# Middle stage of a two-layer attention and expert kernel: shared roots, normalising split over two engines, first rows added by tile

## What is computed

```python
x = x + L0_xattn(layernorm(x), ctx)      # 16 heads of 8, gathered keys
x = x + L0_ffn(layernorm(x))             # one of 16 experts a token, capacity 256
x = x + L1_xattn(layernorm(x), ctx, ctx) # one head, causal, keys = values = ctx
x = x + L1_ffn(layernorm(x))             # dense SiLU layer + product-key experts

def layernorm(x):
    m = mean(x, -1); v = var(x, -1)
    return (x - m) / sqrt(v + 1e-5)
...
scores = einsum('bqd,bkd->bqk', query, key) * 128 ** -0.5
scores = where(tril, scores, -inf)
out = einsum('bqk,bkd->bqd', softmax(scores), value)
```

## Time and profile before

| | us |
|---|---|
| median of 3 runs | 533.6 (532.41 to 536.13) |
| the profiled execution | 534.3 |
| its span in the trace | 532.6 |
| busy TensorE, VectorE | 415.9 (78%), 376.3 (71%) |
| busy ScalarE, GpSimd | 348.5 (65%), 344.5 (65%) |
| mean granted TensorE clock | 0.885 of full speed |

### The profile page before, as it was taken

The page is one execution under the profiler, slowest core; times in us unless marked ns, Lnnn a source line. Parts: engine busy times, 40 slices in busy tenths (PEclk is TensorE's granted clock), DMA queues, the critical chain, the costliest instruction groups (busy, mean ns, idle before and its releaser), DMA issues.

```text
span 532.6 us, 9386 instructions
## 1 busy us (share of the span) xinstructions
PE 415.9 (78%) x2528; PEld 344.0 (65%) x2528; DVE 376.3 (71%) x1628; ACT 348.5 (65%) x652; POOL 344.5 (65%) x251
## 2 busy tenths in 40 slices
PE   4968897819999639788667878889778787888956
PEld 3757786509999528676456657767566665776746
DVE  4457777402232147985989999999999999999970
ACT  2362654412222226986888889988898888998884
POOL 5226777740000175630789888898888988889882
PEclk9796889769999955865989998898999999889897
DMA  7981010023777111100000000000000000000000
GB/s 208 335 219 55 21 35 21 31 74 85 217 195 214 39 55 37 54 26 1 11 10 21 10 20 10 20 20 10 20 10 20 20 10 20 10 20 20 10 11 11
DMA packets 42418, 29.71 MB, mean 56 GB/s; under 512 B 4155, under 2 KB 38555, under 8 KB 42395
## 3 DMA queue, kind: packets, MB, share of 16 engines
q1 hardware_dynamic: 38539, 22.85, 14.9%
q0 software_dynamic: 2624, 6.30, 3.5%
q10 hardware_dynamic: 1232, 0.31, 0.3%
HBM read 18.95 MB, written 8.39 MB: 51 GB/s over the span
## 4 chain that ended last, share of the span: by engine, by line
DVE 22%; POOL 15%; ACT 12%; issue 5%; PE 4%; DVEq 1%; ACTq 0%; POOLq 0%
POOL arena_sb L484 15%; DVE picked_sb L1408 10%; ACT arena_sb L720 7%; ACT L720 4%; DVE bank L1370 2%; DVE first_sb L1367 2%; PE bank L1052 1%; DVE best_sb L1396 1%; DVE first_sb L1372 1%; DVE near_sb L1375 1%; DVE arena_sb L1421 1%; ACT xh_sb L510 1%; DVE pair_sb L1391 1%; ACT sc_sb L646 1%; PE bank L981 1%
## 5 line engine op out<-in xcount | busy, mean ns | idle before, releaser
L484 POOL TENSOR_TENSOR arena_sb<-arena_sb,picked_sb 128x2192 f32<-128x2192 f32 x32 | 154.4, 4846 | 25.6 <-DVE picked_sb L1408 25.6
L1408 DVE SCALAR_TENSOR_TENSOR picked_sb<-arena_sb,best_sb,bank 128x36 f32<-128x36 f32 (+1 forms) x256 | 107.7, 493 | 1.2
L1052 PE MATMUL bank<-ident_sb,arena_sb 128*128 128x128 f32 (+1 forms) x512 | 73.2, 305 | 34.6 <-DVE arena_sb L1421 30.9
L1052 PEld LDWEIGHTS bank<-ident_sb,arena_sb 128*128 128x128 f32 (+1 forms) x512 | 66.6, 169 | 39.8 <-issue 28.2
L476 POOL TENSOR_TENSOR arena_sb<-near_sb,sim_y_sb 128x1536 f32<-128x1536 f32 x32 | 87.7, 2759 | 1.3 <-DVE near_sb L1375 1.3
L720 ACT ACTIVATE arena_sb<-arena_sb,bsum_sb 128x548 f32<-128x548 f32 x128 | 85.6, 740 | 1.0 <-POOL arena_sb L484 0.8
L449 POOL DMA_INDIRECT picked_sb<-made,made_row_sb x32 | 30.7, 961 | 78.9 <-DMA made<-arena_sb 70.0
L714 ACT ACTIVATE arena_sb<-arena_sb 128x2192 f32<-128x2192 f32 x32 | 65.3, 2042 | 0.2
L1043 PE MATMUL bank<-w_down_t_sb,h_sb 128*128 128x128 f32 x256 | 34.8, 280 | 16.0 <-DVE x_all_sb L1427 15.3
L1043 PEld LDWEIGHTS bank<-w_down_t_sb,h_sb 128*128 128x128 f32 x256 | 31.1, 192 | 18.9 <-issue 18.9
L1031 PEld LDWEIGHTS bank<-xt_sb,w_up_t_sb 128*128 128x128 f32 x256 | 33.5, 192 | 14.8 <-issue 14.8
(11 more groups left out here) (176 smaller groups left out, 866.0 us busy)
## 6 DMA issues: line engine op xcount, KB each, us to landing
w_sb<-w SPq DMA_DIRECT2D x32, 256.0 KB, 3.4
...
```

The costliest lines, as they stand in the source:

```text
L484: pool.tensor_tensor(pp[p][:, :, :], pp[p][:, :, :], picked[p][:, :, :], ALU.mult).then_inc(weighed, 1)
L1052: ins = pe.matmul(bank[4 * p][0:n, c * P:(c + 1) * P], pp[p][:, h, c * P:c * P + n], ident[:, :], is_transpose=True, start=h == 0, stop=h ...
L1408: ins = dve.scalar_tensor_tensor(out=picked[p][:, h, lo:hi], in0=vv[p][:, h, lo:hi], scalar=best[p][:, h, TOP - 1:TOP], in1=scores, op0=AL ...
```

## The change

- `combine(0)` waits tile by tile, on a semaphore for each of the first four gathers (`first_gathered`).
- Means, variances and roots of statistics 2 (block g) and statistics 3 (block g-2) lie side by side in `cmv` and `croot`, eight columns. `roots(g)` makes both with one logarithm and one exponential over 128x8 and signals `croot_ready`. It waits for `cstat2_ready` of g and `cstat3_ready` of g-2. The factor 128^-0.5 of `cscale` has gone into `centre_s`, a scaled copy of `centre` which the contexts are multiplied with.
- `last_tokens(g)` on ScalarE normalises tiles 0 and 1; a new `last_tokens(g)` on GpSimd makes the bias and then tiles 2 and 3 (`cxh_pool`). It stands where `biases3(g)` stood. PE's `last_tokens_t(g)` waits for both.

```diff
-        cbias, cscale, cve2, cve3, crstd, cnb = ([sb(f"{n}{p}", [P, BT]) for p in two] for n in "cbias cscale cve2 cve3 crstd cnb".split())
+        cmv = [sb(f"cmv{p}", [P, TT, 2]) for p in two]
+        croot = [sb(f"croot{p}", [P, TT]) for p in two]
+        cmv2, cmv3 = ([t[:, lo:lo + BT] for t in cmv] for lo in (0, BT))
+        cscale, crstd = ([t[:, lo:lo + BT] for t in croot] for lo in (0, BT))
...
-            step(pool.memset(eps_d[:, :], EPS * D))
             step(pool.tensor_scalar(centre[:, :], ident[:, :], -1.0 / D, None, ALU.add))
+            step(pool.tensor_scalar(centre_s[:, :], centre[:, :], float(D) ** -0.5, None, ALU.mult))
...
-            def biases3(g):
+                                            ).then_inc(first_gathered[n] if g == 0 else gathered[g], 16)
+
+            def last_tokens(g):
+
                 p = g % 2
-                pool.wait_ge(croot3_ready, g + 1)
+                pool.wait_ge(croot_ready, g + 3)
                 if g >= 2:
                     pool.wait_ge(cxh_ready, g - 1)
                 step(pool.tensor_tensor(cnb[p][:, :], cmv3[p][:, :, 0], crstd[p][:, :], ALU.mult))
                 pool.tensor_scalar(cnb[p][:, :], cnb[p][:, :], -1.0, None, ALU.mult).then_inc(crstd3_ready, 1)
+                hold(pool, crstd3_ready, g + 1)
+                if g >= 2:
+                    pool.wait_ge(xt3_mm, g - 1)
+                for t in range(BT // 2, BT):
+                    ins = pool.tensor_scalar(xh[p][:, t, :], x_all[:, g * BT + t, :], crstd[p][:, t:t + 1], cnb[p][:, t:t + 1],
+                                             ALU.mult, ALU.add)
+                ins.then_inc(cxh_pool, 1)
...
-                biases3(g)
+                last_tokens(g)
                 if g + 4 < NB:
                     gathers(g + 4)
...
-            def normalise(first, dst, scale, bias, done):
-                for t in range(BT):
+            def normalise(first, dst, scale, bias, done, tiles=BT):
+                for t in range(tiles):
                     ins = act.activation(dst[:, t, :], x_all[:, first + t, :], ACT.Identity,
...
-            def roots2(g):
+            def roots(g):
 
                 p = g % 2
-                act.wait_ge(cstat2_ready, g + 1)
-                step(act.activation(cve2[p][:, :], cmv2[p][:, :, 1], ACT.Ln, bias=eps_d[:, 0:1], scale=float(D)))
+                lo, hi = 0 if g < NB else BT, TT if g >= 2 else BT
+                if g < NB:
+                    act.wait_ge(cstat2_ready, g + 1)
                 if g >= 2:
+                    act.wait_ge(cstat3_ready, g - 1)
                     act.wait_ge(cbias_ready, g - 1)
-                act.activation(cscale[p][:, :], cve2[p][:, :], ACT.Exp, scale=-0.5).then_inc(crstd2_ready, 1)
-
-            def roots3(g):
-                p = g % 2
-                act.wait_ge(cstat3_ready, g + 1)
-                step(act.activation(cve3[p][:, :], cmv3[p][:, :, 1], ACT.Ln, bias=eps1[:, 0:1]))
-                if g >= 2:
-                    act.wait_ge(crstd3_ready, g - 1)
-                act.activation(crstd[p][:, :], cve3[p][:, :], ACT.Exp, scale=-0.5).then_inc(croot3_ready, 1)
+                if g >= 4:
+                    act.wait_ge(crstd3_ready, g - 3)
+                    act.wait_ge(cxh_pool, g - 3)
+                step(act.activation(croot[p][:, lo:hi], cmv[p][:, lo:hi, 1], ACT.Ln, bias=eps1[:, 0:1]))
+                act.activation(croot[p][:, lo:hi], croot[p][:, lo:hi], ACT.Exp, scale=-0.5).then_inc(croot_ready, 1)
 
             def exps(g):
                 p = g % 2
-                act.wait_ge(crstd2_ready, g + 1)
+                hold(act, croot_ready, g + 1)
...
-                normalise(g * BT, xh[g % 2], crstd[g % 2], cnb[g % 2], cxh_ready)
+                normalise(g * BT, xh[g % 2], crstd[g % 2], cnb[g % 2], cxh_ready, BT // 2)
...
             for g in range(NB - 2):
-                roots3(g)
-                roots2(g + 2)
+                roots(g + 2)
                 last_tokens(g)
...
                 probabilities_out(g + 2)
-            roots3(NB - 2)
+            roots(NB)
...
-            roots3(NB - 1)
+            roots(NB + 1)
...
-                pe.matmul(bank[(0, 2, 3, 4, 6)[n]][:, 0:hi - lo], centre[:, :], ctx_row[:, lo:hi],
+                pe.matmul(bank[(0, 2, 3, 4, 6)[n]][:, 0:hi - lo], centre_s[:, :], ctx_row[:, lo:hi],
...
+                pe.wait_ge(cxh_pool, g + 1)
...
-                dve.wait_ge(gathered[g], 16 * BT)
+                if g:
+                    dve.wait_ge(gathered[g], 16 * BT)
                 for n in range(g * BT, g * BT + BT):
+                    if g == 0:
+                        dve.wait_ge(first_gathered[n], 16)
                     ins = dve.scalar_tensor_tensor(out=tile(n), in0=made_x[:, n, :], scalar=gate[:, n:n + 1],
...
-                    dve.wait_ge(crstd2_ready, g - 1)
+                    dve.wait_ge(croot_ready, g - 1)
...
-                dve.wait_ge(crstd2_ready, g + 1)
+                dve.wait_ge(croot_ready, g + 1)
```

More of the change, by code:

```diff
@@ L102, in program @@
         eps1 = sb("eps1", [P, 1])
-        eps_d = sb("eps_d", [P, 1])
+        centre_s = sb("centre_s", [P, P])
         arena = sb("arena", [P, 4, HP * WIDE])
@@ L214, in program @@
         cc_mm, cc_ready = sem("cc_mm"), sem("cc_ready")
-        (x2_ready, cstat2_ready, crstd2_ready, cstat3_ready, crstd3_ready, cxnt_mm, cxnt_ready, csc_mm, cmax_ready, cbias_ready, cexp_ready, cpt_mm,
-         cpt_ready, co_mm, x3_ready, croot3_ready) = map(sem, (
-            "x2_ready cstat2_ready crstd2_ready cstat3_ready crstd3_ready cxnt_mm cxnt_ready csc_mm cmax_ready cbias_ready cexp_ready cpt_mm "
-            "cpt_ready co_mm x3_ready croot3_ready").split())
+        (x2_ready, cstat2_ready, cstat3_ready, crstd3_ready, cxnt_mm, cxnt_ready, csc_mm, cmax_ready, cbias_ready, cexp_ready, cpt_mm,
+         cpt_ready, co_mm, x3_ready, croot_ready, cxh_pool) = map(sem, (
+            "x2_ready cstat2_ready cstat3_ready crstd3_ready cxnt_mm cxnt_ready csc_mm cmax_ready cbias_ready cexp_ready cpt_mm "
+            "cpt_ready co_mm x3_ready croot_ready cxh_pool").split())
+        first_gathered = [sem(f"first_gathered{t}") for t in range(BT)]
         (down_mm, xt3_mm, xt3_ready, cxh_ready, sim_mm, sim_ready, score_mm, up_mm, h1_ready, near_ready, vv_ready,
@@ L668, in _ @@
             tokens_out(0)
-            roots2(0)
+            roots(0)
             exps(0)
@@ L672, in _ @@
             probabilities_out(0)
-            roots2(1)
+            roots(1)
             exps(1)
```

3 lines of the change are left out of this document (1 added, 2 removed).

## The result

| | before | after |
|---|---|---|
| median of 12 runs each | 534.06 us (531.37 to 536.13) | 536.56 us (534.02 to 538.90) |
| ratio | 1 | 1.0047, 95% interval 1.0028 to 1.0067 |
| profiled execution, its span | 534.3, 532.6 | 534.24, 532.5 |
| first gather to the last stage's first VectorE instruction | 67.06 | 68.02 |
| from there to the end | 280.83 | 279.71 |

The changed kernel is 2.5 us slower: inside 1%, where 535.5 us was forecast, and with an interval that excludes 1. The two profiled executions do not show it in their spans. The one of after is 2.3 us quicker than its own median, so it is the stage that has to be read, not the span.

The account below looks back on a forecast made before the run. No engine was taken as full; gathers arrive nearly just in time, so GpSimd's added work shows. Late gathers +2.9 less the tail's 0.9 make +2.0 us on the 533.6 median: 535.6, rounded to 535.5, range 532.3 to 539.2.

Parts of the forecast that it names:

- First rows: Start of the middle stage: block 0 taken tile by tile, so combines 1 to 3 come 0.78 us earlier.
- The constant: One added GpSimd product of 0.55 us ahead of the first barrier, 0.5 us of it hidden.
- The tile: GpSimd's two normalising products a turn, ahead of the gathers: 0.55 us each, plus 0.1 wait on its own bias.
- The landing: From a group's last gather issue to its block's combine: between 2.46 and 3.38 us, taken as 3.0.
- GpSimd's issues: Gather issues behind root, bias and tiles: GpSimd's own turn 6.77 us against 6.31, two-turn loop through the root 14.15.
- Sum at the gathers: Combines in the middle stage come late: block 4 by 1.2 us, block 6 by 2.4, block 7 by 2.9.
- The tail: After the last gather: 0.45 us back at block 7's maximum, 0.48 at block 6's last tokens, together 0.9.
- The last stage: Its first VectorE instruction comes near 253.8 us; the rest of the span, 280.8 us, stays unchanged.
- The shared root: ScalarE saves 0.43 us a turn and waits 0.62 for the bias; with 0.77 of tiles off, 0.58 freer.
- A: Rival: gathers are not late, with tiles of 0.35 us and landings of 2.5; -0.5 us, 533.1; chance 0.20.
- B: Rival: VectorE's sequence alone bounds the middle stage's turn, 6.0 us instead of 6.31; -2.9 us, 530.7; chance 0.07.
- C: Rival: GpSimd's tiles cost 1.0 us each, by contention with VectorE, its turn 7.67; +5.9 us, 539.5; chance 0.11.

Follow-up runs that it names:

- e9: The changed kernel unaltered, measured again as a reference: 536.13 us, ratio 1.0036.
- e1: The kernel before with only the first rows waited for tile by tile: 534.18 us, ratio 0.9995.
- e3: The kernel before with only half of the last normalising moved to GpSimd, two roots kept: 533.96 us, ratio 1.0001.
- e12: The changed kernel with GpSimd's half from block 4 on only, last tokens behind the exponentials, similarities first at the seam: 536.41 us, ratio 1.0034.
- e2: The kernel before with only the shared root and scaled constant, all four tiles on ScalarE: 536.89 us, ratio 1.0062.
- e5: The changed kernel with all four tiles normalised on ScalarE, none on GpSimd: 545.75 us, ratio 1.0025 within its set.
- e4: The changed kernel with gathers issued two tiles further ahead: 535.20 us, ratio 1.0035.

## Why the prediction was right, and where not

The time came out in the range, 1.1 us above the forecast. The likeliest case was the one that happened: late gathers, in every one of blocks 4 to 7. That the number came so near is luck in part. The sum put +2.0 us into the middle stage; in the profile this stage grew by 1.02, while the medians moved by 2.5. And one of its signs of being wrong, that the second start moves and the end does not, holds in the profiled execution (252.79 against 251.77, span 532.5 against 532.6); the medians and e9 say that the end does move. By its steps:

- *First rows.* Block 1 was said at 196.5 and was added at 196.54; 0.78 us, as e1 shows alone.
- *The constant.* 0.55 said, 0.549 measured. GpSimd's constants ended at 6.27 us and PE started at 6.57, still held by a load. Hidden.
- *The tile.* 0.55 taken, 0.477 in the mean of 16. The wait on its own bias was 0.21, not 0.1. So wait and pair, said at 1.20, took 1.10 (0.21 and 0.89) to 1.24 (0.21 and 1.03). In the first turn the gather behind took 1.13 instead of 1.02.
- *The landing.* 3.0 taken, 2.45 to 2.48 measured: the term most mis-sized, 0.5 us too high at each block.'s 3.38 was a real landing, but the rarer one: of the 20 additions of blocks 4 to 7 in all profiles that waited for a gather, 17 came 2.45 to 2.60 us after its issue and three later, at 3.38 (before), 3.27 (e3) and 3.18 (e12).
- *GpSimd's issues.* The last ones of groups 4 to 7 were said, by the sum, at 214.0, 220.8, 228.15 and 234.9, and came at 214.13, 220.73, 227.88 and 234.48. So the chain through root, bias, tiles and issues was right to 0.4 us. Two of its terms were somewhat high: GpSimd's own turn took 6.60 us, not 6.77, and the loop of two turns through the root 13.75, not 14.15.
- *Sum at the gathers.* Block 4 said at 217.0, came at 216.60; block 6 231.15 and 230.36; block 7 237.9 and 236.93. +2.9 said, +1.92 measured, and the landing explains half of the difference. Waits of 0.5 to 1.2 us were said and 0.23 to 0.74 came.
- *The tail.* 0.9 back, and 1.92 - 1.02 = 0.90 came. The maximum of block 7 waits 0.18 instead of 0.63, the 0.45 of the step.
- *The last stage.* Said near 253.8, came at 252.79. The rest was said unchanged at 280.8 and took 279.7; in e1 to e12 it lies between 279.6 and 280.8 us, so 1 us of a single profiled span is scatter. The stage's +1.0 and e9's +1.6 us are less than the medians' +2.5 (and +2.2 in e9); 0.7 to 1.5 us is not located.
- *The shared root.* The sum had its way through GpSimd to the gathers, which is the one that acts in the changed kernel. Its way through ScalarE and PE was missing. The prediction counted 0.43 off ScalarE, 0.62 of waiting on, and let both act only on GpSimd's chain and on ScalarE's sum ("so 0.58 us freer"). It did not follow the exponentials, PE's order and the scores behind the last tokens. Alone the root costs 0.62% (e2). In the changed kernel the half takes 0.77 us of tiles off ScalarE: the exponentials start at 209.59, 0.50 behind the addition, as in the kernel before. e5, without the half, has e2's waits back. e4, without the late gathers, still has waits of up to 1.59 at the maxima. The sum came near for this reason too, not only for those it gave: the half happened to pay what the sum had left out.

Of the rivals, A (gathers in time) had the landing right and GpSimd's turn wrong: its tile of 0.35 was too cheap. B fell with the turn. GpSimd's 6.78 was said as 6.77, but that is chance: it is the mean of two turns of 6.60 and one of 7.15 in which the root was waited for. C's price was not reached: no pair of tiles took over 1.33 us. Its mechanism, contention, is there: the pair took 0.88 or 0.89 us away from VectorE's addition of rows, beside it 1.01 to 1.03, and that addition 1.25 to 1.31 instead of 1.13. Beside VectorE's addition of the attention, which reads one of its inputs from PSUM (`bank`), neither grew:

```profile
243.20 0.89 POOL L469 TENSOR_SCALAR xh_sb<-x_all_sb,croot_sb,cnb_sb 128x128 f32<-128x128 f32 x2 [0.21 <-POOL cnb_sb L464]
...
243.24 1.12 DVE L1348 SCALAR_TENSOR_TENSOR x_all_sb<-bank,csum_sb,x_all_sb 128x128 f32<-128x128 f32 x4
```

That is in accord with the Trainium skill's GPSIMD Engine Reference (8. Key points), which names a VectorE instruction with two SBUF inputs as one case of contention. The Trainium skill's GPSIMD Engine Reference (3.1 Elementwise) gives about 0.35 us for a tile, an estimate from its cycles an element; the measured 0.44 to 0.48 decides.

The range's upper end, 539.2, was said to lie half of the way from 538 to C's 539.5; that would be 538.75. Nothing hangs on it here.
